# Text LayerNorms of a fused image and text embedder: weights and biases centred once, variance from squares, one scaling and one sum

## The reference, cut to what matters

```python
L, H, D, F = 4, 8, 64, 256
for i in range(L):
    q = heads(x @ Wq[i] + bq[i]); k = v = heads(x @ Wv[i] + bv[i])
    o = softmax(q @ k.T / sqrt(8)) @ v
    y = o @ Wo[i] + bo[i]
    x = x + layer_norm(y, ln1_g[i], ln1_b[i])
    h = gelu(x @ W1[i] + b1[i])
    y = h @ W2[i] + b2[i]
    x = x + layer_norm(y, ln2_g[i], ln2_b[i])
return layer_norm(x, fin_g, fin_b)
# layer_norm: (y - mean(y)) * rsqrt(mean((y - mean(y))**2) + 1e-5) * g + b, over 64 channels
```

## Time and profile before

| | us |
|---|---|
| median of 3 runs (lowest, highest) | 2802.8 (2796.26, 2811.0) |
| span of the profiled execution | 2797.4 |
| busy PE, PEld | 2344.6 (84%), 1847.9 (66%) |
| busy DVE, ACT, POOL | 1922.6 (69%), 1461.9 (52%), 1242.9 (44%) |

### The profile page before, as it was taken

One profiled execution on the slowest core, in us unless ns is written; L12 is line 12 of the kernel. 1 busy time (PEld: TensorE's weight loads), 2 busy tenths in 40 slices (PEclk: granted clock), 3 DMA queues, 4 the chain that ended last, 5 costly groups with the idle time before them and its releaser, 6 DMA issues. The chain is left out here.

```text
span 2797.4 us, 63303 instructions
## 1 busy us (share of the span) xinstructions
PE 2344.6 (84%) x19769; PEld 1847.9 (66%) x19769; DVE 1922.6 (69%) x6555; ACT 1461.9 (52%) x3500; POOL 1242.9 (44%) x1650
## 2 busy tenths in 40 slices
PE   6699999688877888699877887189989898699998
PEld 5699999666665666577656666167666666466665
DVE  3455555468856886677767885676676777488888
ACT  2122222146665665655575666565565656566664
POOL 2233333146555664655574655633333333343442
PEclk8899999779988998899988998585686868699999
DMA  4100000000000000000000000000000000000000
GB/s 116 28 17 11 17 11 6 1 2 0 0 1 2 1 0 1 2 1 0 1 1 2 0 0 1 1 1 0 0 0 0 0 0 0 2 10 9 9 9 11
DMA packets 38122, 19.09 MB, mean 7 GB/s; under 512 B 28045, under 2 KB 37389, under 8 KB 37903
## 3 DMA queue, kind: packets, MB, share of 16 engines
q1 hardware_dynamic: 38003, 17.64, 2.5%
HBM read 14.27 MB, written 3.36 MB: 6 GB/s over the span
## 5 line engine op out<-in xcount | busy, mean ns | idle before, releaser
L444 PE MATMUL im_c<-im_a_hi,im_w 128*128 128x256 f32 (+2 forms) x1920 | 429.6, 318 | 46.9 <-POOL im_a_lo L341 46.9
L444 PEld LDWEIGHTS im_c<-im_a_hi,im_w 128*128 128x128 f32 x1920 | 321.5, 191 | 63.2 <-POOL im_a_lo L341 47.6
L1012 POOL TENSOR_TENSOR tx_KB<-tx_KF,tx_head_rows 128x1248 fp32r<-128x1248 f32 x128 | 288.1, 2271 | 52.3 <-DVE tx_KF L881 52.3
L444 PE MATMUL im_c<-im_a_lo,im_w 128*128 128x256 f32 (+2 forms) x960 | 304.2, 317 | 0.0
L830 POOL TENSOR_TENSOR tx_rstd<-tx_var_eps,tx_power 77x4 f32<-77x4 f32 x128 | 130.7, 1021 | 365.1 <-DVE tx_var_eps L826 365.1
L1080 ACT ACTIVATE tx_PT<-tx_scores_t 77x624 f32<-77x624 f32 x256 | 174.6, 682 | 221.2 <-PE tx_scores_t L1224 216.0
L1224 PE MATMUL tx_scores_t<-tx_QP,tx_KB 128*77 128x78 f32 x2048 | 202.7, 251 | 8.9 <-DVE tx_QP L901 3.1
L895 DVE TENSOR_REDUCE tx_mpad<-tx_scores 77x8 fp32r<-77x616 f32 x256 | 202.1, 790 | 9.7 <-PE tx_scores L1206 9.3
L334 POOL TENSOR_TENSOR im_rstd<-im_var_eps,im_power 128x4 f32<-128x4 f32 x64 | 68.7, 1073 | 305.7 <-DVE im_var_eps L262 305.7
L1224 PEld LDWEIGHTS tx_scores_t<-tx_QP,tx_KB 128*77 128x77 f32 x2048 | 184.2, 158 | 28.8 <-DVE tx_QP L901 28.8
L837 ACT ACTIVATE tx_yn<-tx_y,tx_neg_mean_rstd,tx_rstd 77x64 f32<-77x64 f32 x512 | 188.9, 433 | 7.1 <-POOL tx_neg_mean_rstd L832 7.1
(11 more groups left out here) (287 smaller groups left out, 6212.7 us busy)
## 6 DMA issues: line engine op xcount, KB each, us to landing
im_x<-x SPq DMA_DIRECT2D x16, 384.0 KB, 3.3
out<-h_img SPq DMA_DIRECT2D x32, 64.0 KB
tx_toks<-x_txt SPq DMA_DIRECT2D x1, 1925.0 KB
im_raw<-L_tok_conv_w SPq DMA_DIRECT2D x1, 1280.0 KB, 8.7
out<-h_txt SPq DMA_DIRECT2D x32, 38.5 KB
im_raw<-L_tok_conv_w SPq DMA_DIRECT2D x1, 960.0 KB, 4.9
im_raw<-L_tok_conv_w SPq DMA_DIRECT2D x1, 640.0 KB, 6.0
tx_raw_W<-L_txt_W SPq DMA_DIRECT2D x2, 256.0 KB, 6.2
```

Of the source, the lines that this page charges most:

```text
L444: last = pe.matmul(acc[:, :, d0:d1], w[c][:, slot, part], img[:, b0_:b1_, d0 + shift:d1 + shift, kj:kj + J], start=opens, stop=closes)
L1012: pool.tensor_tensor(KB[:, par, t], KF[:, t].bitcast(F32).unsqueeze(1).broadcast_to([P, HPT, QW]), head_rows[:].unsqueeze(2).broadcast_to( ...
```

## The change

1. **Setup**, once: DVE takes the mean over the 64 output channels out of Wo, bo, W2 and b2 of all four layers. Wo and bo are kept twice beside each other: centred, and centred times ln1_g. High and low parts of bo and b2 go into rows 0 and 32 of new weight sections; a tile of ones is added.
2. **PE**: `project_o` starts with one matmul of ones against the bias, 512 columns wide, and its eight matmuls are 128 columns wide in place of 64. `down` starts with one of 256 columns and takes the banks `tx_maxT` and `work[1]` in turn. K and Q projections swap `work[0]` and `work[1]`.
3. **ACT**: the four `ln_norm` activations go; one Square out of PSUM over the quad comes (`ln_square`), at b = 3, and in the feed-forward step ahead of gelu.
4. **DVE**: bias add, bn_stats, bn_aggr and the negated mean go. `ln_var` sums the squares and makes the variance; `ln_apply` multiplies what lies in PSUM by rstd, in the attention step at b = 0. The gain product and the sum of the first norm go from DVE; the second norm keeps both.
5. **POOL**: the product mean times rstd goes; `mid_sum`, one sum of 77x256, comes for the first norm, between `cut` of `os` and `split_k`.
6. **Waits**: PE frees `work[1]` on `y_scaled` (after `ln_apply`) in place of `y_set`; `project_v` waits for the fourth `cut_qk` of the quad in place of the third.
7. Image and text branch each end with their semaphores cleared and a barrier over all engines.

```diff
+        def ln_square(act, n, par, centred):
+            act.wait_ge(y_made, n + 1)
+            act.activation(square[:, par], centred, ACT.Square).then_inc(y_squared, 1)
+
+        def ln_var(dve, n, par):
+            dve.wait_ge(y_squared, n + 1)
+            dve.tensor_reduce(square_sum[:, par], square[:, par], AX.X, ALU.add).then_inc(y_summed, 1)
+            dve.wait_ge(y_summed, n + 1)
+            dve.tensor_scalar(var_eps[:, par], square_sum[:, par], 1.0 / D, EPS, ALU.mult, ALU.add).then_inc(y_var, 1)
...
             pool.tensor_tensor(rstd[:, par], var_eps[:, par], power[0:R], ALU.pow).then_inc(y_rstd, 1)
-            pool.wait_ge(y_rstd, n + 1)
-            pool.tensor_tensor(neg_mean_rstd[:, par], neg_mean[:, par], rstd[:, par], ALU.mult).then_inc(y_scale, 1)
+
+        def ln_apply(dve, n, par, y_psum):
+            dve.wait_ge(y_rstd, n + 1)
+            dve.tensor_tensor(yn[:, par], y_psum, rstd[:, par].unsqueeze(2).broadcast_to([R, QUAD, D]), ALU.mult)\
+                .then_inc(y_scaled, 1)
...
                             elif not first:
                                 normalise_o(n * QUAD - 1, 1 - par, QUAD - 1)
+                            if b == 0 and not at_most(g, 1):
+                                ln_apply(dve, ln - 1, par, y_att[:, :, 1])
...
-                            if b == 2 and not at_most(g, 1):
-                                ln_sum(dve, ln - 1, par, g - 2, "ln1_g")
-                            if b == 3 and first:
+                            if b == 3:
                                 join_second()
                             if b == 3 and not first:
-                                ln_stats(dve, ln, 1 - par, y_rows, "bo", between=join_second)
+                                ln_var(dve, ln, 1 - par)
...
                             cut(o_rows[:, 1 - par], os_, o_hi, o_cut, n - 1)
+                        if not at_most(g, 1):
+                            mid_sum(pool, ln - 1, par, g - 2, n - 2)
...
-                    pe.wait_ge(qk_cut, n * 4 + 3)
+                    pe.wait_ge(qk_cut, n * 4 + 4)
...
                     pe.wait_ge(*bank_ready)
+                    at, end = SEC["bo"]
+                    pe.matmul(work[1][0:R], ones[:], w[:, at:end].unsqueeze(1).broadcast_to([P, QUAD, 2 * D]),
+                              start=True, stop=False)
...
                                 pe.wait_ge(xT_set, n + 2)
+                                project(n + 1, 0)
                                 if first or isinstance(g, int) and g == 1:
                                     pe.wait_ge(v_set, n + 1)
                                 else:
-                                    pe.wait_ge(y_set, ln)
-                                project(n + 1, 0)
+                                    pe.wait_ge(y_scaled, ln)
                                 project(n + 1, 1)
...
                             pe.wait_ge(xT_set, n + 2)
-                            pe.wait_ge(y_set, norm_at(l, g, True) + 1)
+                            pe.wait_ge(y_scaled, norm_at(l, g, True) + 1)
                             for i in range(2):
                                 project(n + 1, i)
...
         image_branch(p, x, of("L0_tok_", IMAGE_WEIGHTS), ident, h_img, [text, attention, expert])
+        p.end_stage()
+        p.begin_stage()
         text_branch(p, text, ident, h_txt)
+        p.end_stage()
```

More of the change, by code:

```diff
@@ L808, in norm_at @@
             return l * (2 * U) + (U if ff else 0) + g
[L812 to L825, removed]
-            dve.tensor_scalar(var_eps[:, par], mean_var[:, :, 1], EPS, None, ALU.add).then_inc(y_var, 1)
+        y_att = work[1][0:R].rearrange("p (b c d) -> p b c d", b=QUAD, c=2)
+        y_ff = [bank[0:R, 0:QUAD * D].rearrange("p (b d) -> p b d", b=QUAD) for bank in (max_bank, work[1])]
+        def ln_square(act, n, par, centred):
[6 more added lines that the diff above has]
+            dve.tensor_scalar(var_eps[:, par], square_sum[:, par], 1.0 / D, EPS, ALU.mult, ALU.add).then_inc(y_var, 1)
         def ln_scale(pool, n, par):
@@ L983, in feed_forward @@
                             set_cols(l + 1)
-                        ln_stats(dve, ln, par, y_rows, "b2")
+                        ln_var(dve, ln, par)
+                        if not first:
+                            ln_apply(dve, ln - 1, 1 - par, y_ff[1 - par])
+                            end_sum(dve, ln - 1, 1 - par, g - 1, n - 1)
                         if last:
+                            ln_apply(dve, ln, par, y_ff[par])
                             dve.wait_ge(w_set, l * 5 + 7)
@@ L1122, in attention @@
                                 hi(o_rows[:, 1 - par], os_, o_hi)
-                            if b < 2 and not at_most(g, 1):
-                                ln_norm(act, ln - 1, par, (2 * b, 2 * b + 1))
                             if b == 2 and not last2:
@@ L1187, in project @@
                     for part in range(2):
-                        last = pe.matmul(work[(i + 1) % 2][:, 0:QW], sec(m, part, t * P, (t + 1) * P),
+                        last = pe.matmul(work[i % 2][:, 0:QW], sec(m, part, t * P, (t + 1) * P),
                                          xT[:].rearrange("p b s -> p (b s)"), start=part == 0, stop=part == 1)
@@ L1266, in down @@
                     pe.wait_ge(f_gelu, n + 1)
-                    pe.wait_ge(y_set, ln)
+                    pe.wait_ge(y_scaled, ln - 1)
+                    at, end = SEC["b2"]
+                    pe.matmul(y_ff[par], ones[:], w[:, at:end].unsqueeze(1).broadcast_to([P, QUAD, D]),
+                              start=True, stop=False)
                     for b in range(QUAD):
                         for half in range(2):
-                            last = pe.matmul(work[1][0:R, b * D:(b + 1) * D],
+                            last = pe.matmul(y_ff[par][:, b],
                                              HT[:, par, half].rearrange("p (b s) -> p b s", b=QUAD)[:, b, 0:R],
-                                             w2[:, half], start=half == 0, stop=half == 1)
+                                             w2[:, half], start=False, stop=b == QUAD - 1 and half == 1)
                     last.then_inc(y_made, 1)
```

176 lines of the change are left out of this document (115 added, 61 removed).

## The result

The changed kernel takes 2880.8 us (median of four runs, 2873.9 to 2888.8) against 2806.9 for the kernel before: a ratio of 1.028, with a 95% interval of 1.023 to 1.032. It is slower, inside the range given and 26 us under the forecast of 2907. The profiled execution took 2874.7 us with a span of 2872.9, against 2797.4 before.

The account below looks back on a forecast made before the run. The prediction took a ring of hand-overs between engines, neither PE nor DVE full, as the bound. Terms 88 - 4 - 2 + 11 + 7 + 4 = +104 on 2797.4 give 2901; plus 5.4, 2907 us; range 2835 to 2940.

Parts of the forecast that it names:

- The walk through the step: Attention step traced through engine queues from the start of `score_t`: next step at 14.8 us, 1.7 us more per step.
- The attention term: Attention loop, 52 steps at 1.7 us more each: +88 us (+57 to +109).
- transitions to feed-forward: Where attention meets feed-forward: 0.5 gained behind ACT's norms, as much lost to wider `project_o`; -2 us in all (-8 to +4).
- The bias matmul: Attention step on PE: the added 512-column bias matmul costs 0.25 us (bounds 0.2 and 0.6).
- The feed-forward step: Feed-forward loop: 0.18 us wait behind ACT's `ln_norm` goes, bias matmul adds 0.13; -4 us over 56 steps (-12 to +8).
- Feed-forward to attention: Joint to attention: PE's first projections wait 3.3 us longer; net +2.8 us a layer, +11 us (+4 to +14).
- Setup and clearing: Text setup's extra operations, +7 us (+5 to +10); clearing semaphores with two barriers, +4 us (0 to +8).
- The sum: All terms over the whole program: 88 - 4 - 2 + 11 + 7 + 4 = +104 us.
- Relief wins: Attention step: DVE's power wait covered, `ln_sum` gone before `find_max`; if `ln_apply` ends by t = 2.5; about 2783; chance 0.10.
- Half the delay: Attention step: later parts swallow what is lost at b = 0; +0.5 us a step, about 2845; chance 0.13.
- Square's own table: ACT in both loops: square needs table loads of 1.28 us, 256 of them, up to +328, about 3235; chance 0.02.
- The clock: Attention step: PE's clock falls in new 1.6 us stalls; 3 us more on half the steps, about 2985; chance 0.05.

Follow-up runs that it names:

- e7: Changed kernel with four Identity activations of 77 x 64 put back on ACT in the feed-forward step, results unused: 2897.3 us, ratio 1.035 to before.
- e8: e3 with DVE's `ln_apply` also ahead of `normalise_o` at b = 0: 2743.5 us, ratio 0.970 to before (0.982 by medians of all runs).
- e1: Changed kernel with DVE's variance moved ahead of the fourth sample's join of maxima: 2811.4 us, ratio 1.004 to before.
- e6: Kernel before with one added 77 x 256 sum on POOL ahead of its cut of K, result unused: 2790.3 us, ratio 0.997 to before.
- e3: Changed kernel with variance ahead of the fourth join on DVE and POOL's `mid_sum` behind `split_k`: 2760.8 us, ratio 0.985 to before.
- e9: e3 run again, on the same chip as e8: 2774.7 us, ratio 0.991 to before.
- e5: Kernel before with only a wait added: PE's second K projection waits for the variance's power and scaling: 2906.6 us, ratio 1.038 to before.
- e10: Changed kernel with PE's wait filled by repeating the next quad's first K projection, eight matmuls more: 2918.6 us, ratio 1.045 to before.

## Why the prediction was right, point by point

**The walk through the step held to 0.13 us.** Counted from the start of `score_t` at 665.88, the forecast and the trace are: variance done 2.9 and 2.78; power 4.0 and 3.87; scaling done 4.45 and 4.32; second K pair at 4.5 and 4.38; cut of `os` done 6.7 and 6.69; sum 7.4 and 7.38; `split_k` 11.9 and 11.83; scores 12.0 and 11.89; next step 14.8 and 14.72. The waits it named are in the rows: DVE 0.67 us for POOL's power, PE 1.46 us for DVE, the scores 0.57 for `split_k`. The cover of ACT's square is there too: it takes 0.38 and ends well before DVE turns to it.

**The attention term** was +88 for 52 steps and the transitions to feed-forward -2, together +86; the two rows of the table give 92.2 - 4.8 = +87. That agreement is luck: two errors of the forecast cancel in it. The thirteenth interval of each layer, which the table counts with the transition, carries the loss too (49.2 us in the four layers before, 57.3 after), so 52 steps cost 92.2 + 8.1 = +100. About 86 of that is at full clock (48 x 1.64 and four times 1.93); the rest is steps at a lower clock, for which the forecast had no term. And the transition proper gave back 13, not 2. PE's idle time in it fell from 3.75 to 3.27 us, as forecast, but the interval that holds it, 16.5 us in all four layers before at a granted clock of 0.54 to 0.59, took 12.9 to 13.3 in three of them at 0.73 to 0.74, and 15.7 in the fourth at 0.56. Most of the 13 goes with the clock, then, and why it stayed higher is not shown.

**The bias matmul**: 0.25 forecast with eight wider matmuls in it. L1312 starts 0.30 before L1316, and without it the step is 0.23 shorter.

**The feed-forward step was mis-sized**: -4 forecast, -20.3 measured. I gave the end of ACT's norms 0.18 us less 0.13 for the bias matmul. The bias matmul costs 0.17 (861.83 to 862.00), but with `xTf` ready in time `up` overlaps the end of `down`: 0.31 a step. I took a wait's length for the whole of its price, and left out the overlap that the wait also breaks. e7 gives back 13.4 of the 20.3; of the other 7, 5.3 lie in the second interval of the four loops (4.95 us before, 3.4 to 3.9 after), which e7 leaves short.

**Feed-forward to attention**: +2.8 a layer forecast, +11 for four; but there are only three joints between layers, and they took +2.8 together, 0.9 each. PE does wait for the scaling (4.36 us), and the product and sum beside `split_k` take 2.19 and 2.37. But the 3.68 us of issue in the earlier trace rows did not come again: L936 starts right behind L929. I had added it as a fixed cost, and it was none; what it was, no run here tells. The 2.19 and 2.37 us, for products that took 0.42 elsewhere, agree with the lock that the Trainium skill, "SBUF — State Buffer", section on the two sides of SBUF, describes for DVE operations with two SBUF inputs beside a GpSimd operation that reads SBUF; after the last layer, where no `split_k` runs, the same L902 took 0.41.

**Setup and clearing**: +7 and +4 forecast. From DVE's first clear of the text setup to its first of the layers is 39.77 us, 7.65 more than before. The first of these instructions starts 1.28 us later, which takes in the first clearing of semaphores with its barrier. These two make +8.9 of the +10.0. The second clearing, behind the final text norm, shows in POOL's timeline:

```profile
1888.20 0.72 POOL L1474 TENSOR_TENSOR h_txt<-tx_yn,tx_fin_b 77x256 f32<-77x256 f32 x1 [1.30 <-DVE tx_yn L1450]
1890.03 0.33 POOL L1662 MEMSET at_V<- 128x272 f32 x1 [1.11 <-POOLq L60]
```

From the first start to the second it is 1.83 us, and was 1.03 before, so 0.8 us for this clearing and its barrier: about 2 in all where I took 4.

**The sum**: +104 forecast for the span, +75.5 measured. The 28 between them are the feed-forward steps (16), the joints between layers (8), the untouched code at the end (4) and what is left of the small terms.

**The rivals.** Relief wins: its condition was a scaling done by t = 2.5; it came at 4.32. e8 came close to that condition by order alone: there PE's four K matmuls start at t = 2.35 and the scaling at 2.30. Half the delay: the step would be 13.6; it was 14.73. Square's own table: ACT loads tables seven times in the text layers, as before, and the squares took 0.38 us each. The clock: it did fall, in about half of the steps as that rival had it, but the long steps cost 22 us in all over 48 usual ones, not 3 us each (next section but one). The row that spoke against it, was one of four: at another layer's end in the same trace of before the same idle time was followed by the 1.2 GHz level:

```profile
1157.44 1.11 PE L1179 MATMUL tx_work<-ident,tx_xs 128*128 128x128 f32 x4 [2.15 <-POOL tx_xs L1005]
```

## What to carry to other kernels

When an operation that frees a buffer is moved behind a longer chain, the price is the chain as seen by the engine that refills the buffer; read it by walking the queues, not from the busy times, which here fell on two engines while the time rose. Before giving such a change up, look along the new chain for operations that stand in a queue behind something they don't need: three reorderings turned a loss of 2.8% into a gain of about 2% here. And an operation's cost depends on what else holds up the engine at the end of its chain: the same sum on POOL cost 0.04 us a step in one kernel, where DVE had work to do meanwhile, and 0.68 in the other, where DVE stood waiting.

## What I had not expected of the hardware

In the changed kernel 23 of 48 attention steps were over 0.4 us longer than the usual one. The clock fell in more of them, 35; in some of these the step still took 14.73 us, at a mean granted clock of 0.88. TensorE's timeline in the longest of them, 17.60 us with a granted clock of 0.71:

```profile
714.88 0.56 PE L1249 MATMUL tx_work<-tx_xT,tx_w 128*128 128x312 f32 x2 [1.48 <-DVE tx_yn L887]
715.27 0.68 PE L1285 MATMUL tx_scores_t<-tx_QP,tx_KB 128*77 128x78 f32 x8
...
716.76 1.09 PE L1249 MATMUL tx_work<-tx_xT,tx_w 128*128 128x312 f32 x4
...
717.93 1.32 PE L1285 MATMUL tx_scores_t<-tx_QP,tx_KB 128*77 128x78 f32 x8
...
725.68 1.22 PE L1316 MATMUL tx_work<-tx_w,tx_oT 128*77 128x128 f32 x8
...
727.25 0.50 PE L1267 MATMUL tx_scores<-tx_KB,tx_QF 128*77 128x312 f32 x2
```

From about 717 to 727 each group takes nearly twice its time at full clock (1.32 for 0.77, 1.22 for 0.70): the 1.2 GHz level. It begins two microseconds after an idle stretch of 1.48, with work between, and ends while the work goes on. The count goes with the kernel: 19 to 29 long steps of 48 in each of the seven profiles whose usual step is 14 us or more, three in the kernel before and in e1, ten in e6, none in e3, e8 and e9. All of the seven have the wait for the scaled y (e5: for the power) at its full length but one, e10, where it is filled. So what lowers the clock there is open. It was not tried to add idle time elsewhere in a kernel whose step is short.

Code that no version touches, after the last variance, took between 1012 and 1045 us in these profiles, with the same instructions. Half a per cent on this kernel is therefore shown by its runs together, and the terms are better read from the intervals of a repeated instruction.
